# A four-stage image network on one core: the hourglass stage in sixteen 32x32 tiles, with layouts by image and by strip in turn

## The reference, cut to what matters

```python
y = get_operator(x)                  # five edge filters
y = maxpool2(conv3x3(y, conv1))      # -> 64x64      (an earlier stage)
y = maxpool2(conv3x3(y, conv2))      # 64x64 -> 32x32 (from here on: the hourglass stage)
y = maxpool2(conv3x3(y, conv3))      # -> 16x16
y = deconv2x2(conv3x3(y, conv4))     # -> 32x32
y = deconv2x2(conv3x3(y, conv5))     # -> 64x64
y = deconv2x2(conv3x3(y, conv6))     # -> 128x128
y = conv3x3(y, conv7)
return orig * y                      # orig: the normalised x; x is added to it
```

## Time and profile before

| | |
|---|---|
| median of three runs | 21,136.5 us |
| profiled execution | 21,070.2 us, span of its core 21,068.6 us |
| mean granted TensorE clock | 0.912 of full speed |
| hourglass stage | from about 19,145 us to the end |
| one group of it | about 472 us |

### The profile page before, as it was taken

One profiled execution on the slowest core, in us unless ns is written; L12 is line 12 of the kernel. 1 busy time (PEld: TensorE's weight loads), 2 busy tenths in 40 slices (PEclk: granted clock), 3 DMA queues, 4 the chain that ended last, 5 costly groups with the idle time before them and its releaser, 6 DMA issues. The chain is left out here.

```text
span 21068.6 us, 398582 instructions
## 1 busy us (share of the span) xinstructions
PE 16924.9 (80%) x141144; PEld 7118.2 (34%) x141144; DVE 14859.5 (71%) x15523; ACT 12935.7 (61%) x23178; POOL 10507.4 (50%) x6534
## 2 busy tenths in 40 slices
PE   6888888888853888888888849999999436668999
PEld 2333333333321222222222215555555212223444
DVE  8999999999942788888888836666656248882111
ACT  6989889989931666666666628878878013331111
POOL 5877777777710677777777720000000347771000
PEclk9999999999976999999999969989989768889999
DMA  2000000000045000000000041211111775552111
GB/s 73 12 12 11 12 12 11 12 12 11 12 122 138 17 18 18 18 18 18 17 18 18 16 91 25 37 36 34 34 36 33 190 184 109 108 106 53 43 43 40
DMA packets 1504668, 964.38 MB, mean 46 GB/s; under 512 B 761016, under 2 KB 1329824, under 8 KB 1492264
## 3 DMA queue, kind: packets, MB, share of 16 engines
q1 hardware_dynamic: 1358488, 732.04, 15.6%
q10 hardware_dynamic: 118480, 117.04, 2.2%
q0 software_dynamic: 26624, 100.67, 1.7%
HBM read 733.84 MB, written 215.64 MB: 45 GB/s over the span
## 5 line engine op out<-in xcount | busy, mean ns | idle before, releaser
L323 DVE TENSOR_TENSOR l_mx<-l_p_v,l_puN 128x2048 f32<-128x2048 f32 x2560 | 5637.0, 2278 | 154.2 <-PE l_p_s L538 141.7
L538 PE MATMUL l_p_s<-l_mx,l_w2z 128*32 128x512 f32 x32768 | 3838.2, 613 | 582.2 <-ACT l_mx L450 320.2
L343 POOL TENSOR_TENSOR l_mx<-l_pv,l_puP 128x2048 f32<-128x2048 f32 x1024 | 3715.6, 3645 | 326.8 <-PE l_p_s L538 321.1
L1249 DVE TENSOR_TENSOR_SCAN l1m_hs<-l1m_da,l1m_carry,l1m_pu 128x512 f32<-128x512 f32 x2304 | 2823.7, 1267 | 114.0 <-issue 12.6
L1907 ACT ACTIVATE l1d_ab<-l1d_pt 128x1024 f32<-128x1024 f32 x2304 | 2299.0, 1025 | 699.2 <-PE l1d_pt L1661 672.7
L1298 POOL TENSOR_TENSOR l1m_hc<-l1m_hs,l1m_cs 128x1024 f32<-128x1024 f32 x1152 | 2709.9, 2352 | 9.2 <-DVE l1m_hs L1249 5.7
L469 ACT ACTIVATE l_mx<-l_pv,l_puP 128x128 f32<-128x128 f32 x8192 | 2447.1, 394 | 0.8
L1785 DVE TENSOR_SCALAR l1d_hat<-l1d_ab 128x1024 f32<-128x1024 f32 x2304 | 1623.8, 705 | 803.6 <-ACT l1d_ab L1907 483.3
L538 PEld LDWEIGHTS l_p_s<-l_mx,l_w2z 128*32 128x32 f32 x32768 | 986.9, 112 | 3031.3 <-issue 1779.3
L1239 DVE TENSOR_TENSOR l1m_pu<-l1m_pu,l1m_bs 128x512 f32<-128x512 f32 x2304 | 1476.9, 687 | 746.7 <-PE l1m_pu L994 746.7
L450 ACT ACTIVATE l_mx<-l_mx 128x2048 f32<-128x2048 f32 x1024 | 1954.8, 1909 | 48.0 <-POOL l_mx L343 47.2
(11 more groups left out here) (336 smaller groups left out, 24604.5 us busy)
## 6 DMA issues: line engine op xcount, KB each, us to landing
n_xt<-x_after SPq DMA_DIRECT2D x48, 2048.0 KB
l3a_xs<-x_after SPq DMA_DIRECT2D x384, 256.0 KB, 5.2
l3a_xe<-x_after SPq DMA_DIRECT2D x480, 96.0 KB, 2.1
l1m_sq<-seq SPq DMA_DIRECT2D x256, 144.0 KB
n_xt<-in_x_dram SPq DMA_DIRECT2D x16, 2048.0 KB
l_xs<-in_x_dram SPq DMA_DIRECT2D x128, 256.0 KB, 2.8
x_after<-l_ot SPq DMA_DIRECT2D x128, 256.0 KB, 2.4
l1d_xr<-x_after POOLq DMA_DIRECT2D x32, 1024.0 KB, 10.0
```

The source lines that it names most:

```text
L323: v.tensor_tensor(mx[:, r % QB, :, :, :], columns.unsqueeze(1).broadcast_to([P, 4, G, P]), rows.broadcast_to([P, 4, G, P]), ALU.max).then_ ...
L343: g.tensor_tensor(mx[:, r % QB, :, :, :], pv[:, u, :, :].unsqueeze(1).broadcast_to([P, 4, G, P]), rows.broadcast_to([P, 4, G, P]), ALU.add ...
L538: ins = pe.matmul(p_s[R * q:R * (q + 1), 512 * u:512 * (u + 1)], w2z[:, 31 - r:63 - r], mx[:, r % QB, q, :, :].rearrange("p t v -> p (t v) ...
L1249: dve.tensor_tensor_scan(hs[:, p % 3, part, :], da[:, p % 3, part, :], pu[:, LC * bank:LC * (bank + 1)], carry[:, u, c:c + 1], ALU.mult, A ...
```

## The change

Four things change, all in `hourglass`.

1. conv2, conv6 and conv7 are made by `convolve_tiles` and deconv3 by `spread_tiles`: for each tap, 16 matmuls with 32x32 weights, one per pair (row group r, column group c). Four chunks ("quad") come from 144 matmuls instead of 36, or 16 instead of 4 for deconv3. Each quad begins with one small 32x32 matmul that carries the wait for four banks.
2. The layouts alternate. Row group r of the result lands in bank r, column group c on partitions 32c. Conv2 reads strips (16 rows of 64, with a halo row on each side) on partition groups and writes images on partition groups; conv6 reads images and writes strips; deconv3 the reverse; conv7 reads images and writes strips. So `in2`, `up3`, x and the result are now by strip: strip h on partitions 32h on, the four images side by side in the free dimension.
3. A load or store of x is now four DMAs of 32 partitions, each partition moving two pieces of 512 elements (2 KB) where it moved one of 1024 (4 KB). `in2` is 16 DMAs of 17 or 18 rows instead of one of 64. The normalising activation is split in two, since a unit now holds two images per partition group with their own scale.
4. `BANKS` is 8. Conv6, conv2, deconv3 and conv7 are unrolled on TensorE; deconv2's chunks use the eight banks. The layers between keep their block-diagonal matmuls.

```diff
-    BANKS = 4
+    BANKS = 8
...
-        in2 = m.sb("in2", [P, S1 + 2, S1 + 2])
+        in2 = m.sb("in2", [P, IM, S1 // 4 + 2, S1 + 2])
...
-        up3 = m.sb("up3", [P, S1, S1])
+        up3 = m.sb("up3", [P, IM, S1 // 4, S1])
...
+        strips = lambda a: a.rearrange("(g v e) c (h q i) w -> h g v q c e (i w)", v=2, e=2, h=4, i=4)
...
+        def of_unit(a, h, g, j, u):
+
+            return a[h][at(g), u % 2, at(j * (XB // 2) + u // 2), :, :, :].rearrange("g q c e n -> (g q c) e n")
...
-                sp.dma_start(in2[:, 1:S1 + 1, 1:S1 + 1], fg[at(g), :, :].rearrange("g p (h w) -> (g p) h w", w=S1)).then_inc(in2_load, 16)
+                for h in (1, 0, 2, 3):
+                    for i in range(IM):
...
+                        sp.dma_start(in2[T * h:T * (h + 1), i, row:row + hi - lo, 1:S1 + 1],
+                                     first[at(g * IM + i), :, lo:hi, :].rearrange("b c h w -> (b c) h w")).then_inc(in2_load, 16)
...
+                        for h in (1, 0, 2, 3):
+                            sp.dma_start(of_unit(og, h, g, j, u), xt[T * h:T * (h + 1), u].rearrange("p (e y) x -> p e (y x)", e=2)).then_inc(stored[u], 16)
...
+            def start_of(g, name, quad):
+
+                bank_free(g, name, 4 * quad, 3)
+                pe.matmul(bank(name, 4 * quad, T)[0:T, :], wc[:, 0, 0, 0:T], wc[:, 0, 0, T:2 * T], start=True, stop=True, tile_position=(0, 0))
+
+            def convolve_tiles(g, name, k, quad, window):
+
+                start_of(g, name, quad)
+                for tap in range(9):
+                    for c in range(4):
+                        for r in range(4):
+                            ins = pe.matmul(bank(name, 4 * quad + r)[T * c:T * (c + 1), :], wc[T * r:T * (r + 1), k, tap, T * r:T * (r + 1)],
+                                            window(r, c, tap // 3, tap % 3), start=tap == 0, stop=tap == 8, tile_position=(T * r, T * c))
+                            if (tap, c) == (8, 3):
+                                ins.then_inc(product_done, 1)
...
-                with pe.Fori(0, H // 4 // BANKS) as j:
-                    pe.wait_ge(act_took, taken_before(g, "conv7", "a") + BANKS)
-                    for u in range(BANKS):
-                        convolve(g, "conv7", 5, in7, W, 512 // W, j * BANKS, u)
+                pe.wait_ge(act_took, taken_before(g, "conv7", "a") + BANKS)
+                for quad in range(8):
+                    convolve_tiles(g, "conv7", 5, quad,
+                                   lambda r, c, dy, dx: in7[T * r:T * (r + 1), 32 * c + 4 * quad + dy:32 * c + 4 * quad + dy + 4, dx:dx + W])
...
-                        act.activation(ht[:, u % 2], xt[:, u], ACT.Identity, scale=gcur[:, 0:1], bias=gcur[:, 1:2]).then_inc(h_ready, 1)
+                        for e in range(2):
+                            i, rows = 2 * (u % 2) + e, slice(4 * e, 4 * e + 4)
+                            ins = act.activation(ht[:, u % 2, rows], xt[:, u, rows], ACT.Identity, scale=gcur[:, i, 0:1], bias=gcur[:, i, 1:2])
+                        ins.then_inc(h_ready, 1)
```

More of the change, by code:

```diff
@@ new lines, in spread_tiles @@
+            def spread_tiles(g, name, k, quad, tap, window):
+                start_of(g, name, quad)
+                for c in range(4):
+                    for r in range(4):
+                        ins = pe.matmul(bank(name, 4 * quad + r)[T * c:T * (c + 1), :], wd[T * r:T * (r + 1), k, tap, T * r:T * (r + 1)],
+                                        window(r, c), start=True, stop=True, tile_position=(T * r, T * c))
+                        if c == 3:
+                            ins.then_inc(product_done, 1)
@@ L2564, in spread @@
             def spread(g, name, k, src, rows, j, tap):
                 bank_free(g, name, j * 4, tap)
-                pe.matmul(bank(name, tap), wd[:, k, tap, :], src[:, at(j * rows, rows), :], start=True, stop=True).then_inc(product_done, 1)
+                pe.matmul(bank(name, 4 * j + tap), wd[:, k, tap, :], src[:, j * rows:(j + 1) * rows, :], start=True, stop=True).then_inc(product_done, 1)
             with pe.Fori(0, NG) as g:
-                with pe.Fori(0, S1 // 8 // BANKS) as j:
-                    pe.wait_ge(in2_load, g * 16 + 16)
-                    for u in range(BANKS):
-                        convolve(g, "conv2", 0, in2, S1, 512 // S1, j * BANKS, u)
+                pe.wait_ge(in2_load, g * 256 + 256)
@@ L2574, in _ @@
+                for quad in range(2):
+                    convolve_tiles(g, "conv2", 0, quad,
+                                   lambda r, c, dy, dx: in2[T * r:T * (r + 1), c, 8 * quad + dy:8 * quad + dy + 8, dx:dx + S1])
                 pe.wait_ge(in3_ready, g + 1)
@@ L2645, in _ @@
                         add_bias(g, "deconv2", 4 * j, tap, places(in6, S1)[:, tap // 2, tap % 2, rows * j:rows * (j + 1), :],
[L2646 to L2654, removed]
+                                 product("deconv2", 4 * j + tap).rearrange("p (h w) -> p h w", w=S2), 7)
+                for u in range(8):
+                    add_bias(g, "conv6", 0, u, up3[:, u % 4, 8 * (u // 4):8 * (u // 4) + 8, :],
+                             product("conv6", u).rearrange("p (h w) -> p h w", w=S1), 4)
+                for u in range(32):
+                    strip, tap, half = u % 4, u // 4 % 4, u // 16
+                    rows = slice(16 * strip + 8 * half, 16 * strip + 8 * half + 8)
+                    add_bias(g, "deconv3", 0, u, places(in7, H)[:, tap // 2, tap % 2, rows, :],
+                             product("deconv3", u).rearrange("p (h w) -> p h w", w=S1), 8)
                 act.wait_ge(gcur_ready, g + 1)
```

49 lines of the change are left out of this document (23 added, 26 removed).

## The result

On one chip, four executions each, the median went from 21,145.0 to 20,090.8 us: the ratio is 0.951, with a 95% interval of 0.947 to 0.955. The profiled execution took 20,118.0 us (span 20,116.1), where the one before took 21,070.2. The median is inside the range of 20,070 to 20,480, but 177 us under the forecast of 20,268; it is nearest to the rival "instructions arrive in time" (20,124).

A forecast was written before the change was run, and what follows sets the result against it. TensorE was taken to bound the hourglass, 401 of about 472 us a group. The terms sum to -210.8 us a group, -843 in four; from an average of 21,111 this gives 20,268 us, range 20,070 to 20,480.

The forecast's parts named there:

- instructions arrive in time: Rival: instruction packets are not held back, a conv7 quad takes 9.86 us, 36 less a group, total 20,124; chance 0.14.
- 1 conv2: conv2 goes from 63.9 to 22.3 us a group, cold start included: -41.6.
- Term 2: Maximum after conv2: last four chunks finish together, +2.1; clock dropped when conv3 starts, +2.6 us a group.
- 4 conv6 and bias after it: conv6 goes from 62.1 to 19.6 us a group, -42.5; more ScalarE work exposed after it, +2.1.
- Term 5: deconv3: ScalarE becomes the limit at 0.73 us a chunk, 24.7 instead of 27.7 us a group: -3.0.
- Term 6: conv7: bursts at l1o's average of 13.6 us because of late instructions, 247.5 to 109 us a group: -138.2.
- Terms 7 and 8: Group end: 5.5 us of VectorE after conv7's last quad, +3.5; in2 load 13.8 to 18 us, +4.2.
- the forecast case: A conv7 quad of 12 to 15 us, total 20,268 us; chance 0.70.
- in2's wait goes over 25 us: Sign that the forecast is wrong; the in2 wait was expected at 15 to 18 us.
- DMA sets the pace: Rival: four DMAs per transfer and slow 2 KB stores stretch a conv7 quad to 16.5 us, total 20,432; chance 0.12.
- Transfers in single file: Rival: a conv7 unit's four DMAs run one after another, 25.2 us a unit, total 21,443; both slower rivals together 0.03.
- The tiles do not overlap: Rival: tiles run four at a time, not sixteen, burst 34.4 us, total 21,330; both slower rivals together 0.03.

The follow-up runs named there:

- experiment 4: Changed kernel plus a 2 MB load of x per group at conv7's start, 16 KB contiguous per partition: hourglass 906.7 us against 910.7.
- experiment 3: Changed kernel plus a 2 MB load of x per group at conv7's start, in 8,192 rows of 256 bytes: hourglass 912.6 us against 910.7.
- experiment 10: Changed kernel plus a 2 MB load per group at conv7's start, long runs, as four DMAs of 32 partitions: hourglass 924.5 us against 910.7.
- experiment 2: Changed kernel with the next group's in2 load issued in mid-conv7, behind the first four units' stores: hourglass 855.8 us against 910.7.
- experiment 9: Changed kernel with conv7's matmuls moving 256 columns instead of 512, same instruction count: hourglass 890.5 us against 910.7.
- experiment 5: Changed kernel with conv7's last three taps left out, a third of its work: hourglass 856.5 us against 910.7.
- experiment 6: Changed kernel with the tile loops exchanged, row group outside and column group inside: hourglass 900.4 us against 910.7.
- (7): Changed kernel with l1o's and l2's image strips loaded as one contiguous run per partition: hourglass 907.1 us, a burst of l1o averages 13.8 us.
- (11): Changed kernel with l1o's and l2's stores issued in SyncE's queue behind the loads: hourglass 906.5 us against 910.7.
- experiment 1: Changed kernel with the next group's in2 load issued before conv7's stores, once conv2 frees the buffer: hourglass 829.0 us against 910.7.

## Why the prediction was right, and where it was wrong

Per group, before to after, against my terms:

| term | forecast | measured |
|---|---|---|
| 1 conv2 | -41.6 | 63.9 to 22.2: -41.7 |
| 2 maximum and cold conv3 | +4.7 | idle 1.6 to 3.4, conv3 15.7 to 17.4: +3.5 |
| 4 conv6 and bias after it | -40.4 | 62.1 to 19.8, idle 1.1 to 2.5: -40.9 |
| 5 deconv3 | -3.0 | 28.9 to 21.7: -7.2 |
| 6 conv7 | -138.2 | 247.5 to 82.5: -165.0 |
| 7 and 8 end of conv7 to next conv2 | +7.7 | 17.4 to 29.6: +12.2 |
| sum | -210.8 | -239 |

The last two rows are means over the three groups that another one follows, the others are the second group. Four groups at -239.6, with the +12 only three times, give -970; the stage lost 969.5. The profiled span lost 952.5, since this stage also began 17 us later in the run after.

The time fell into the range because the range took in the rivals, and not because the forecast case came true: a conv7 quad of 12 to 15 us, to which I gave 0.70, was not seen.

**Term 6 is the step that failed**: "I take 13.6, l1o's". A quad took 10.3 us (82.5 / 8: 9.86, and the slow first burst and a gap spread over eight), 3.3 less, and 8 x 3.3 = 26 us a group is nearly all that the sum is off by. (8 x 13.6 is 108.8 and would be -138.7; the term is written 0.5 us short.) "Issue" gaps were there, with the size taken from the wrong neighbour. I carried an average over from l1o by its DMA share alone. But the share in conv7 came out at 0.57, not 0.6 to 0.85: the 2 KB stores ran at 7.34 MB / (0.284 x 82 us) = 315 GB/s, and not at the 208 of l2's tail. And l1o's loads are of another kind: 2 MB in one go. Experiments 4, 3, 10 and 2 put the gaps in order: 2 MB over 128 partitions in long runs made none, in short rows 1.2 us, by strips 2.2, and 2.3 MB by strips in short rows, later in conv7 beside the x traffic, 3.8 us in each of the three groups that have the load (11.5 / 3). The last one differs in place as well as in form. The gaps are not the whole cost either: experiment 10's 14 us are 7 of gaps and 9 of slower matmuls, less 2 of other waits. Experiment 9 shows why the step is so sharp: the stream has next to no reserve at 4.34 us per 128 MATMULs.

The Trainium skill's page "Runtime: NRT & Kernel Launch", Instruction fetch mechanics, which calls the crossing of a 16 KB boundary mostly hidden, was right for the changed kernel (2.9 us of gaps in 911) and not for experiment 9, where nearly each 128 MATMULs end in a gap, mostly of 1.0 to 2.4 us (81.4 in 890.5). The Trainium skill's page "TensorE: Matmul & The Clock Gate", Part 3, gives 10.6 times for one pack of sixteen tiles; the trace after has 12.7 in streams of 288 MATMULs, so the page's figure doesn't carry over to them.

**Term 5** named the right limit, as the window of deconv3 shows: ScalarE busy 19.98 of 21.5 us. But it priced the activation by its length. The group of its line in that window (count, busy us and mean ns, then idle time before):

```profile
L2653 ACT ACTIVATE l3b_in<-l3b_ps,l3b_bias 128x512 f32<-128x512 f32 x32 | 19.8, 760 | 1.6 <-PE l3b_ps L2593 1.6
```

32 activations of 0.760 us keep ScalarE busy for only 19.8 us: they overlap, and one comes every 0.62 us. The earlier trace rows could not have told this: before, chunks came 0.87 us apart, no two activations touched, and busy time divided by count (116.8 / 160) was the same 0.73 as the mean. The Trainium skill's page "ScalarE: Activation LUTs", What ACT_TABLE_LOAD costs, says that activations back to back overlap by about 93 ns; the trace agrees in kind and shows 140.

**Terms 7 and 8** together were 4.5 us short, most of it in term 8. From the end of conv7 to the first in2 DMA it was 3.3 us and is 7.8 on average (+4.6, forecast +3.5); from there to the last landing 13.8 became 21.7 (+7.9, forecast +4.2). I counted "1 MB of stores and as much of loads" beside in2. It was 1.05 MB of stores, but 2.1 MB of loads, since all four buffers are refilled for the next group at once. 5.5 MB at 183 GB/s are 30 us. In sixteen pieces in2 also costs SyncE 16.1 to 18.6 us of issuing, which the prediction left out; the runs don't part the two causes. One sign of being wrong was "in2's wait goes over 25 us": the load took 20.9 to 23.0 us, but TensorE's wait for it 28.8 to 30.3, so on TensorE's side the sign came.

**Terms 1, 2 and 4** held within 1.2 us. Term 2's lost clock is real, though mostly smaller than its 2.6: after 3.38 us of idling conv3's 36 MATMULs took 17.41 us in three groups and 18.8 in one, where conv5's 36 of the same size take 15.71 each time. The granted clock was 0.57 in conv3's first 4 us in the second group, and 1.00 in conv5's. The small layers stayed.

**The rivals.** "Instructions arrive in time" had a quad at 9.86 us, no lost clock before conv3 and in2 at 15.1; the first nearly came true (10.3), the others not. Its 20,124 is near the median of 20,091 in part by luck: it also leaves out the 4.2 us of term 5. "DMA sets the pace" falls: TensorE waited for no bank in conv7. But experiment 5 shows it 1 us behind, at 8.8 us a quad. "Transfers in single file" falls by the same number: with two units in a quad, that is 4.4 us a unit, where it had 25.2. "The tiles do not overlap" falls by the 9.75 us burst, in both orders of the tiles (experiment 6). The instruction queue carried 126 packets in the stage, 32 a group, as foretold (three before, where the prediction has none):

```profile
q8 instruction: 126, 2.06, 0.9%
```

**What stays open**: why l1o loses as much as 60 us, and with it what holds the instructions back. It is neither its short rows alone (7) nor its second queue (11). The packets themselves are not stretched: by their share of the engines a packet takes 0.014 x 16 x 437 / 86 = 1.1 us in l1o and 0.009 x 16 x 928 / 126 = 1.1 us in the hourglass. So it is their start that is late, and no run shows why. The extra loads in conv7 came after TensorE had idled 3.6 us, so that its first instructions may have been there already; l1o with its image loaded over 128 partitions, or by strips in pieces of other sizes, was not tried.

## What to carry to other kernels

Price a burst by the busy time of its own kind, and a neighbouring stage's average only after asking what its gaps come from: which transfers, how large, over how many partitions, and how long they run. When matmuls get three times faster, look first at what is queued behind them: here a load in program order behind the last stores made TensorE wait 30 us at each of three boundaries, and issuing it earlier gave back 82 us. After such a change, ask of each engine how far it is behind the new limit (here ScalarE 0 in deconv3, the x buffers 1 us a quad in conv7, the instruction stream next to nothing).

## What the runs showed of the hardware

- Sixteen 32x32 tiles in fp32: 33.9 ns a MATMUL at 512 columns, in either order of the tiles (experiment 6), and 21.5 ns at 256 (experiment 9). Halving the columns takes off only 37%.
- Straight code of such matmuls comes in packets of 16 KB, one for 128 MATMULs. Beside 180 GB/s of traffic a step of 128 came every 3.7 to 5.5 us, 4.45 on average (experiment 9).
- The same 2 MB made gaps of 0 to 2.2 us a group on TensorE by the form of the load: long runs over 128 partitions took about 7 us and made none, rows of 256 bytes 10 to 11 us and 1.2, four strips of long runs some 10 us and 2.2 (experiments 4, 3, 10).
- ScalarE's activations of 128x512 follow each other every 0.62 us in deconv3, though each is recorded with 0.76.
- SyncE needed 0.3 to 2.5 us to issue each of the sixteen in2 DMAs, 17 or 18 rows by 32 partitions, 16.1 to 18.6 us in all beside stores and x loads, and 12.0 us where in2 ran alone (experiment 1).
